# One weighting of a unit on GpSimd, the gate product a slice ahead, and the experts' sum in token layout

## The reference, cut to what matters

```python
def _L1_attn_ref(query, ...):                     # 16 heads of 8, attends over the 8 batch rows
    attn = softmax(einsum('nqd,nkd->nqk', q, k) * scale)
    out = einsum('nqk,nkd->nqd', attn, v)
    ...
    return out @ out_w.T + out_b
def _L1_ffn_ref(hidden_states, w_gate, w1_e, w3_e, w2_e, w1_s, w3_s, w2_s):
    weights, idx = _gate(x, w_gate)
    combine = (one_hot(idx, E) * weights[..., None]).sum(1)
    g = silu(einsum('th,efh->tef', x, w1_e))
    u = einsum('th,efh->tef', x, w3_e)
    routed = einsum('tef,ehf,te->th', g * u, w2_e, combine)
    shared = (silu(x @ w1_s.T) * (x @ w3_s.T)) @ w2_s.T
    return routed + shared
x = x + L0_attn(xn) + L0_ffn(xn)
x = x + _L1_attn_ref(xn, ...) + _L1_ffn_ref(xn, ...)
```

## Time and profile before

| | us |
|---|---|
| median of 3 runs (lowest, highest) | 361.42 (361.18, 362.21) |
| time of the profiled execution | 361.42 |
| its span, first to last instruction | 359.6 |
| busy in the span: PE, DVE, POOL, ACT | 303.3, 310.7, 240.2, 186.4 |
| the loop, 159.2 to 359.6: busy PE, DVE, POOL, ACT | 183.6, 180.0, 161.1, 80.5 |

### The profile page before, as it was taken

How to read it: one execution, slowest core, us unless ns; L and a number is a source line. 1 busy time by engine, 2 the same in 40 slices (tenths; PEclk the granted TensorE clock), 3 DMA queues, 4 the chain that set the end, 5 groups by cost and what they waited for, 6 DMA issues and landing times.

```text
span 359.6 us, 4910 instructions
## 1 busy us (share of the span) xinstructions
PE 303.3 (84%) x1371; PEld 215.1 (60%) x1371; DVE 310.7 (86%) x825; ACT 186.4 (52%) x507; POOL 240.2 (67%) x154
## 2 busy tenths in 40 slices
PE   0559786989899887578898999989989899998993
PEld 0336664778677677564555755656657566675652
DVE  5997899987977867949999899898998989989792
ACT  3346665878778577493622534436334362453611
POOL 4186486654736531119879878799888998889651
PEclk9978999999999999899999999999999999999999
DMA  4690000000000000017842416215434263334000
GB/s 140 171 286 1 2 0 1 3 1 0 3 0 3 0 0 3 0 32 165 181 106 78 99 60 147 77 55 150 114 97 110 59 141 86 100 106 124 3 29 29
DMA packets 21304, 24.81 MB, mean 69 GB/s; under 512 B 2533, under 2 KB 12045, under 8 KB 21277
## 3 DMA queue, kind: packets, MB, share of 16 engines
q1 hardware_dynamic: 20232, 24.03, 25.6%
q10 hardware_dynamic: 820, 0.39, 0.4%
q0 software_dynamic: 224, 0.08, 0.1%
HBM read 22.13 MB, written 2.36 MB: 68 GB/s over the span
## 4 chain that ended last, share of the span: by engine, by line
DVE 37%; PE 24%; issue 15%; POOL 12%; ACT 6%; DMA 3%; SPq 1%; ACTq 0%; DVEq 0%; POOLq 0%
PE Q L933 10%; POOL prod_qk L867 8%; PE VN L933 7%; DVE att L1565 3%; DVE hid L1605 3%; DVE sgc L1592 3%; PE T L933 3%; DVE rope_b L1342 3%; DVE rope_a L1340 3%; POOL prod_pv L877 2%; PE T L929 2%; DMA cw<-comb_table 2%; DVE attn L1372 2%; DVE bst L1183 1%; DVE l_sum L1388 1%
## 5 line engine op out<-in xcount | busy, mean ns | idle before, releaser
L877 POOL TENSOR_TENSOR prod_pv<-prob,qkv 128x1024 f32<-128x1024 f32 x32 | 69.5, 2191 | 17.9 <-DVE att L1565 16.6
L867 POOL TENSOR_TENSOR prod_qk<-qkv 128x1024 f32<-128x1024 f32 x32 | 76.2, 2398 | 4.6 <-DVE above L1435 4.6
L933 PE MATMUL VN<-hid,w 128*128 128x512 f32 x144 | 73.7, 593 | 1.5 <-DVE hid L1605 1.5
L933 PE MATMUL Q<-xT_hi,w_hi 128*128 128x512 f32 x72 | 51.4, 714 | 0.3 <-ACT sg L761 0.2
L1551 DVE TENSOR_REDUCE scr<-prod_qk 128x128 f32<-128x1024 f32 x32 | 38.8, 1213 | 5.4 <-POOL prod_qk L867 5.3
L1605 DVE TENSOR_TENSOR hid<-T,sgc 128x512 f32<-128x512 f32 x64 | 43.4, 678 | 0.0
L933 PE MATMUL Q<-bias,ones 128*128 128x400 f32 (+1 forms) x64 | 28.9, 452 | 14.6 <-ACT v_ext L649 7.2
L1565 DVE TENSOR_REDUCE att<-prod_pv 128x128 f32<-128x1024 f32 x32 | 38.3, 1196 | 0.0
L933 PE MATMUL T<-xT_hi,w_hi 128*128 128x512 f32 x72 | 31.0, 431 | 7.2 <-DVE hid L1605 7.1
L761 ACT ACTIVATE ND<-Q 128x512 f32<-128x512 f32 x32 | 18.6, 582 | 34.8 <-PE Q L933 26.2
L761 ACT ACTIVATE VN<-Q 128x512 f32<-128x512 f32 x32 | 18.6, 582 | 33.7 <-PE Q L933 26.2
(11 more groups left out here) (177 smaller groups left out, 746.5 us busy)
## 6 DMA issues: line engine op xcount, KB each, us to landing
cw<-comb_table SPq DMA_DIRECT2D x62, 256.0 KB, 4.6
out_x<-fin SPq DMA_DIRECT2D x8, 256.0 KB, 4.5
x<-in_x SPq DMA_DIRECT2D x2, 256.0 KB, 3.0
wraw<-in_w1T SPq DMA_DIRECT2D x1, 512.0 KB, 4.1
w3raw<-in_w3T SPq DMA_DIRECT2D x1, 512.0 KB, 4.7
w<-in_w2T SPq DMA_DIRECT2D x1, 512.0 KB, 5.7
cw<-comb_table SPq DMA_DIRECT2D x4, 128.0 KB, 3.0
rope_s<-in_c_sin ACTq DMA_DIRECT2D x1, 256.0 KB, 4.8
```

The source lines that it names most:

```text
L867: pool.tensor_tensor(prod_qk[:, t % 2], bc(qkv2[:, TH * half + t, j, 0:D], 1, NB), qkv2[:, :, j, D:2 * D], ALU.mult).then_inc(qk_prod, 1)
L877: pool.tensor_tensor(prod_pv[:, t % 2].rearrange("p (h e) b -> p b h e", e=HD), bc(prob[:, t].rearrange("p h b -> p b h"), 3, HD), qkv2[:, ...
L933: return pe.matmul(o, lhsT, rhs, start=start, stop=stop)
```

## The change

- **GpSimd takes one weighting of a unit.** For the slices `BASE[n] + 1` (`ON_POOL`), Silu goes into a buffer `sg_w` in SBUF, POOL makes `sgc_w = sg_w * cw` (`weighted`), and DVE's `hid` reads that. `weighted` stands in POOL's queue between the first q*k and `less_max`.
- **Silu in place, gates a slice ahead.** Silu writes back into the bank of its gate product, one of three banks `ND0`, `Q0`, `Q1` in turn, and PE makes the gate product of `k + 1` before the up product of `k`.
- **Experts' sum in token layout.** `hid` becomes the stationary operand, in four pieces of 128 tokens, and `w2` the moving one; the sum and the attention's output product lie in one bank (`VK` and `Q2` in turn). The copy `yT` and the four transposes back go. The output bias is added to `x` beforehand by POOL (`biased`, eight additions of 128x512: seven at the head of steps of the front pipeline, the eighth after the first four q*k).
- **The end.** `BASE[7]` is 64 instead of 65; the last unit's steps lie closer together (scores at `p` of -7, -6, -1, 0, output product at 9, residual at 10), its residual and its store go in two halves; the residual of unit 6 moves from `p = 13` to 15.

```diff
-        bout2 = sb("bout2", [P, 1])
+        bout2 = sb("bout2", [P, D])
...
-        SB = (ND0, ND1)
+        GB = (ND0, Q0, Q1)
+        YB = (VK, Q2)
+        def gate_bank(n, s):
+            return GB[(NS * n + s) % 3]
...
-        BASE = (5, 14, 23, 31, 40, 48, 57, 65)
-        LAST = BASE[NSLOT - 1] + 15
+        BASE = (5, 14, 23, 31, 40, 48, 57, 64)
+        LAST = BASE[NSLOT - 1] + 12
+        END = NSLOT - 1
+        ON_POOL = tuple(b + 1 for b in BASE)
...
-            for n in range(NSLOT - 2, NSLOT):
-                store(n)
-                stored_of(n)
+            store(END - 1)
+            j, half = place(END)
+            for h in range(2):
+                sp.wait_ge(fin_ready, END + 1 + h)
...
-                gated = SB[side(n, s)] if s > 0 else sg
-                act.activation(gated[:, :], QB[side(n, s)][:, :], ACT.Silu).then_inc(sg_ready, 1)
+                if s == 0:
+                    after(act, hid_ready, NS * (n - 1) + 1)
+                k = NS * n + s
+                if k in ON_POOL:
+                    after(act, sgcw_ready, ON_POOL.index(k))
+                gated = sg_w if k in ON_POOL else gate_bank(n, s) if s > 0 else sg
+                act.activation(gated[:, :], gate_bank(n, s)[:, :], ACT.Silu).then_inc(sg_ready, 1)
...
-            def yT_evac(n):
...
-                act.activation(yT[:, (n - 1) % 2], tiles(VK), ACT.Identity, bias=bout2[:, 0:1]).then_inc(yT_ready, 1)
...
+            def biased(c):
+                if c == 0:
+                    pool.wait_ge(ld_w2, 64)
+                pool.wait_ge(xn2_ready, 2 * c + 2)
+                pool.tensor_tensor(x[:, c], x[:, c], bc(bout2[:, :], 1, NJ), ALU.add).then_inc(x_biased, 1)
...
+                run(i, 5, biased)
                 run(i, 1, mx_over_scale)
...
             for t in range(TH):
                 product_qk(0, t, 0, 0)
+            biased(NB - 1)
...
+            def weighted(n):
+                k = ON_POOL[n]
+                r = routed_slice(k % NS)
+                pool.wait_ge(sg_ready, k + 1)
+                pool.wait_ge(ld_cw[r // 2], 32 * (k // NS + 1))
+                after(pool, hid_ready, ON_POOL[n - 1] + 1 if n else 0)
+                settle(pool)
+                pool.tensor_tensor(sgc_w[:, :], sg_w[:, :], cw[:, r // 2, r % 2, :], ALU.mult).then_inc(sgcw_ready, 1)
...
                 next_qk(0)
+                weighted(n)
                 less_max(n)
...
-                mm(VK[:, :], w2[:, routed_slice(s) % NS, :], hid[:, s % 3, :], s == 0, s == NS - 1).then_inc(y_ps, 1)
+                for t in range(TH):
+                    o = slice(t * P, (t + 1) * P)
+                    m = mm(YB[n % 2][:, o], hid[:, s % 3, o], w2[:, routed_slice(s) % NS, :], s == 0 and t == 0, False)
+                m.then_inc(y_ps, 1)
...
-                transposes(Q2, lambda t: att[:, t, :], signal=attT_ps)
-            def output_back(n):
-                pe.wait_ge(yT_ready, n + 1)
+                transposes(ND1, lambda t: att[:, t, :], signal=attT_ps)
+            def attention_product(n):
                 pe.wait_ge(attT_ready, n + 1)
                 for t in range(TH):
-                    pe.matmul(Q2[:, t * P:(t + 1) * P], yT[:, n % 2, t, :], ident[:, :], is_transpose=True, start=True,
-                              stop=False)
-                    m = mm(Q2[:, t * P:(t + 1) * P], attT[:, t, :], wout2[:, :], False, True)
+                    o = slice(t * P, (t + 1) * P)
+                    m = mm(YB[n % 2][:, o], attT[:, t, :], wout2[:, :], False, t == TH - 1)
...
+            gate(0, 0)
             for k in range(LAST):
                 n, s = divmod(k, NS)
+                if k + 1 < NSLICE:
+                    gate(*divmod(k + 1, NS))
                 if k < NSLICE:
-                    gate_and_up(n, s)
+                    up(n, s)
...
-                if s > 0:
+                if s > 0 and NS * n + s not in ON_POOL:
                     r = routed_slice(s)
                     dve.wait_ge(sg_ready, NS * n + s + 1)
...
-                V.tensor_tensor(fin[:, n % 2], x[:, TH * half:TH * half + TH, j, :], tiles(Q2), ALU.add)\
-                    .then_inc(fin_ready, 1)
+                parts = 2 if n == END else 1
+                for h in range(parts):
...
-                first = (-4, -3, -2, -1) if u == 0 else (-8, -7, -2, -1)
+                first = (-4, -3, -2, -1) if u == 0 else (-7, -6, -1, 0) if u == END else (-8, -7, -2, -1)
...
-                if p == 13:
+                if p == (10 if u == END else 15 if u == END - 1 else 13):
                     residual(u)
```

More of the change, by code:

```diff
@@ L326, in build @@
         sgc_ready = sem("sgc_ready")
+        sgcw_ready = sem("sgcw_ready")
         hid_ready = sem("hid_ready")
         y_ps = sem("y_ps")
-        yT_ready = sem("yT_ready")
+        x_biased = sem("x_biased")
         qk_prod = sem("qk_prod")
@@ L401, in upto, with weightings @@
             return min(c, NB) if isinstance(c, int) else c
-        SB = (ND0, ND1)
+        GB = (ND0, Q0, Q1)
+        YB = (VK, Q2)
+        def gate_bank(n, s):
+            return GB[(NS * n + s) % 3]
+        def weightings(k):
+            return sum(1 for m in range(k) if m % NS > 0 and m not in ON_POOL)
         NSLICE = NSLOT * NS
-        BASE = (5, 14, 23, 31, 40, 48, 57, 65)
-        LAST = BASE[NSLOT - 1] + 15
+        BASE = (5, 14, 23, 31, 40, 48, 57, 64)
+        LAST = BASE[NSLOT - 1] + 12
+        END = NSLOT - 1
+        ON_POOL = tuple(b + 1 for b in BASE)
         COMB_AT = BASE[1] + 15
@@ L416, in comb_bank @@
         def comb_bank(h):
-            return (T0, Q2)[h]
+            return (T0, ND1)[h]
         def side(n, s):
@@ L505, in spread @@
                     return
-                after(sp, sgc_ready, (NS - 1) * (n - 1) + 2 * q + 2)
+                after(sp, sgc_ready, weightings(NS * (n - 1) + 2 * q + 3) if n > 0 else 0)
+                after(sp, sgcw_ready, sum(1 for m in ON_POOL if m < NS * (n - 1) + 2 * q + 3))
                 settle(sp)
@@ L543, in _ @@
                 slot(n)
-            for n in range(NSLOT - 2, NSLOT):
-                store(n)
-                stored_of(n)
+            store(END - 1)
+            j, half = place(END)
+            for h in range(2):
+                sp.wait_ge(fin_ready, END + 1 + h)
+                settle(sp)
+                ts = slice(TH // 2 * h, TH // 2 * (h + 1))
+                sp.dma_start(ov[:, TH * half + TH // 2 * h:TH * half + TH // 2 * (h + 1), j, :], fin[:, END % 2, ts])\
+                    .then_inc(stored, 16)
+            sp.wait_ge(stored, 16 * (NSLOT + 1))
         def exp_of(act):
@@ L1104, in down @@
                 if s == 0:
-                    after(pe, yT_ready, n)
-                mm(VK[:, :], w2[:, routed_slice(s) % NS, :], hid[:, s % 3, :], s == 0, s == NS - 1).then_inc(y_ps, 1)
+                    after(pe, fin_ready, n - 1)
+                    if n == 1:
+                        pe.wait_ge(r_step, R_MASKED)
+                for t in range(TH):
+                    o = slice(t * P, (t + 1) * P)
+                    m = mm(YB[n % 2][:, o], hid[:, s % 3, o], w2[:, routed_slice(s) % NS, :], s == 0 and t == 0, False)
+                m.then_inc(y_ps, 1)
             def down_two_before(n, s):
@@ L1136, in gate_and_up @@
                 w = slice(at * P, (at + 1) * P)
-                if n == 0 and s == 1:
+                if n == 0 and s == 2:
                     pe.wait_ge(l1_kept, NT)
-                after(pe, sg_ready, NS * n + s - 1)
-                g = QB[side(n, s)]
+                k = NS * n + s
+                if k >= 3:
+                    if (k - 3) % NS == 0 or k - 3 in ON_POOL:
+                        pe.wait_ge(sg_ready, k - 2)
+                    else:
+                        pe.wait_ge(sgc_ready, weightings(k - 2))
+                g = gate_bank(n, s)
                 mm(g[:, :], w1_hi[:, w], hi, True, False)
@@ L1144, in gate_and_up, with up @@
                 mm(g[:, :], w1_lo[:, w], hi, False, True).then_inc(g_ps, 1)
+            def up(n, s):
+                j, half = place(n)
+                hi = xT_hi[:, TH * half:TH * half + TH, j, :]
+                lo = xT_lo[:, TH * half:TH * half + TH, j, :]
+                at = routed_slice(s) % NS
+                w = slice(at * P, (at + 1) * P)
                 after(pe, hid_ready, NS * n + s - 1)
@@ L1583, in weighted @@
             def weighted(n, s, k):
-                if s > 0:
+                if s > 0 and NS * n + s not in ON_POOL:
                     r = routed_slice(s)
                     dve.wait_ge(sg_ready, NS * n + s + 1)
+                    after(dve, hid_ready, NS * n + s - 1)
                     if n == 0 and r == 0:
@@ L1611, in residual @@
                 dve.wait_ge(yback_ps, n + 1)
+                dve.wait_ge(x_biased, NB)
                 dve.wait_ge(fin_free, n + 1)
-                V.tensor_tensor(fin[:, n % 2], x[:, TH * half:TH * half + TH, j, :], tiles(Q2), ALU.add)\
```

(8 more changed lines are left out.)

40 lines of the change are left out of this document (16 added, 24 removed).

## The result

| | before | after |
|---|---|---|
| median (lowest, highest), us | 361.30 (360.89, 362.21) | 366.38 (365.87, 366.71) |
| profiled execution, us | 361.42 | 366.24 |
| its span, us | 359.6 | 364.2 |
| ratio of after to before, 95% interval | | 1.0124 (1.0098 to 1.0149) |

The account below looks back on a forecast made before the run. POOL's queue, with a stretch of DVE's, was taken to bound the loop; 3.3 us lost before the end, 2.1 given back there: span 360.85 plus 1.82 outside makes 362.7 us, 0.35% slower, range 359.8 to 364.8.

Parts of the forecast that it names:

- Cost nothing: Front pipeline: seven bias additions of 1.27 on POOL, ahead of a product for which it idles 4.42, cost 0.
- S7: Start of unit 7's less_max on POOL, the loop's last: forecast at 338.4, against 335.67 before.
- Rival D: Front pipeline pays for the bias: four additions uncovered, 5.1 us more, 367.8 us; chance 0.05.
- rival B: Loop: POOL's weighting costs 1.05 and Silu is never late, 360.5 us; chance 0.19.
- The estimate of 1.12: Loop: POOL's weighting of 512 elements by the Trainium skill's figure, about 1.12 us; the sum would be about 361.8.
- the ring: Loop: chain of waits from one less_max to the next, POOL's queue with a stretch of DVE's; 22.46 us in unit 4.
- rival C: Loop: POOL never closes the ring, less_max follows smax at once in every unit; 4.1 off, 357.3 us; chance 0.12.
- S4: Start of unit 4's less_max on POOL: forecast at 270.3, against 268.32 before.
- rival E: PE's pieces of 128 don't overlap, 1.56 a slice, PE becomes the bound: about 400 us; chance 0.02.
- A: Loop, the forecast itself: POOL's ring takes the weighting, 362.7 us, bounds 360.5 to 364.8; chance 0.62.
- S1: Start of unit 1's less_max on POOL: forecast at 199.8, with DVE's weighting before it starting 0.9 later.
- S0: Start of unit 0's less_max on POOL: forecast at 176.7 instead of 175.36, from one bias addition and the weighting, 1.25 each.

Follow-up runs that it names:

- both edits: The changed kernel with the front's bias addition moved behind the quantised product and every weighting back on VectorE: 358.39 us, ratio 0.9887 to the kernel before.

## Why the prediction was wrong, step by step

**The step that failed** is the one on the bias in the front pipeline, "Cost nothing". It looked for what hides the additions, found POOL's idle 4.42 ahead of the quantised product, and stopped there. That cover was real: in the changed kernel POOL still waits 3.79 for that product's operand. But a queue's idle time covers only what waits in that queue. Nothing was asked about the engine beside it, and there DVE's root of `ss` fell into the addition and ended with it. The measured price is 2.7 us by the trace and 2.9 by moving the additions, where the sum has 0. With 3.15 for the later loop the forecast's 362.7 becomes 365.85; S7 0.16 later, the last `hid` 0.3 later behind it, the end 0.3 shorter and 0.2 more outside of the span give the 366.2 of the profiled execution. That the two misses of 0.3 cancel is luck.

Rival D had the place right (the loop would start later) and gave 367.8, but its mechanism, additions that delay POOL's product, is not what happened, and its price was four times 1.27 instead of five times 0.58. It had 0.05, on POOL's idle time alone. The row that should have raised it, the root of `mv` that takes 0.67 for eight elements beside `rope_ab` while its like takes 0.17, was in the trace of before; in a table of groups it hid behind a mean of 405 ns.

**What held.** The weighting takes 1.28 to 1.30, 1.24 to 1.25 from start to start (taken: 1.25; rival B's 1.05 falls). The estimate of 1.12 falls too. Silu is late by 0.19 to 0.20 in units 1, 2, 4 and 6 (taken: 0.2). POOL closes the ring in every unit, so rival C is out. The 0.60 off DVE turned into waiting: before the q\*k sum of unit 4 DVE stood 2.40, where it stood 1.23 in the earlier trace rows; the forecast had about 1.8. S4 also came 0.65 behind the end of `smax` instead of 0.08, and this and the 0.60 make the 1.17 more. Unit 1 got its microsecond back: the exponential starts 1.1 after S1 instead of 2.1. Eight pieces of a product with `w2` start 0.11 apart, as forecast; from the first start to the last end they take 1.05 (0.89 was forecast from starts alone; the earlier trace rows has 0.86 for the old form). PE has not become the bound, so rival E is out. At the end 5.47 us lie behind the last `hid`, forecast 5.75. One bound was loose: A's 360.5 does not have the shorter end in it; with its 0.55 less it is 359.9, about the lower end of the range.

**What came out, with its reason only half shown.** S1 was made 0.9 later on the ground that S0 is later by the eighth addition and the weighting, and the distance from S0 to S1 came out as forecast (23.1). In the old loop the ground holds: with the bias alone S0 is 0.97 later and S1 0.96. In the new loop, without the weighting, it does not: there the addition moves S0 by 0.44 and S1 by nothing. So the later S1 of the changed kernel can't be put down to the addition; the weighting without the addition was not tried.

**Where rival C went.** Its 4.1 us off is what both edits leave of the change: 1.1%, or 4.1 us. That does not make its mechanism right: C had POOL close the ring nowhere, and with both edits it still does in units 3 and 5. The gates a slice ahead, the token layout and the new end gain the 1.1% together, and no run separates them; the weighting and the bias, as placed, cost more than that (2.4%).

## What to carry to other kernels

When work goes to another engine's idle time, check two things: that the queue has the gap, and what the neighbouring engine issues in that gap; an instruction of DVE that ends at the same moment as one of POOL, at several times its usual length, may well be held by it, as here. Read single durations, not the mean of a group, to see that. And an operation on a ring costs by its place in the queue: a weighting of 1.29 us in each of eight units cost 5.1 us in all ahead of `less_max`, and nothing between two products of which the second waits for another engine anyway.

## What the runs showed of the hardware that I had not expected

An instruction of POOL in progress held some instructions of DVE to its end, short as they were: 12 elements took 0.75 instead of 0.17 us. The profile books it as duration, not as a wait. Held were `tensor_scalar` from SBUF to SBUF (beside an addition: 0.75; beside a fill: 1.53) and `scalar_tensor_tensor` with both inputs in SBUF (beside an addition: 0.74; beside a fill: 0.17, so not held). Not held were the statistics' `BATCH_NORM_AGGREGATE` (0.64 for eight beside `rope_ab`) and the products with one operand in PSUM, `hid` at 0.63 to 0.69 throughout the loop.

The Trainium skill has this rule: "SBUF — State Buffer", section "SBUF: two separate sides", says that VectorE and GpSimd share one pair of ports, held for a whole instruction by whichever starts first, and that on VectorE's side it concerns operations in a 2-port mode, which it says `tensor_scalar` can enter, and those with two SBUF inputs (these only against GpSimd work that reads SBUF). The four numbers of what was held and not held in these two forms agree with it, the clause in brackets included; they show only VectorE waiting, never GpSimd.
